# AdaLN block with attention: the scale product in column blocks, and the first projections accumulated by pairs of column tiles

## The reference

```python
mod = (_silu(L0_c) @ L0_wmod).reshape(4, 6, 1, -1)
sa, ca, ga, sb, cb, gb = (mod[:, i] for i in range(6))
ga = (2 * (ga >= 0) - 1) * jnp.maximum(jnp.abs(ga), 0.25)   # gb likewise
h = _layernorm(x, axis=-1) * (1 + ca) + sa
qkv = h @ Wqkv + bqkv                                       # 1024 -> 3 * 256
attn = softmax(q k^T / 16); out = (attn @ v) @ Wo + bo      # one head of 256
x = x + ga * out
h = _layernorm(x, axis=-1) * (1 + cb) + sb
x = x + gb * (h @ (weight + lora of this b).T + bias)       # 1024 -> 1024
```

## Time and profile before

| | us |
|---|---|
| median of 3 runs | 1041.43 (1040.65 to 1043.12) |
| the profiled execution | 1042.57 |
| its span in the profile | 1040.8 |
| TensorE busy | 1011.5 |
| VectorE busy | 663.6 |
| ScalarE busy | 309.2 |
| GpSimd busy | 231.2 |

### The profile page before, as it was taken

One profiled execution on the slowest core, in us unless ns is written; L12 is line 12 of the kernel. 1 busy time (PEld: TensorE's weight loads), 2 busy tenths in 40 slices (PEclk: granted clock), 3 DMA queues, 4 the chain that ended last, 5 costly groups with the idle time before them and its releaser, 6 DMA issues.

```text
span 1040.8 us, 12891 instructions
## 1 busy us (share of the span) xinstructions
PE 1011.5 (97%) x5158; PEld 831.6 (80%) x5158; DVE 663.6 (64%) x827; ACT 309.2 (30%) x460; POOL 231.2 (22%) x182
## 2 busy tenths in 40 slices
PE   4899999999999999999999999999999999999996
PEld 1677777888888889888898888888887888888885
DVE  4866756498744398532976548776688578566622
ACT  1422333123232132420234523322432333142300
POOL 0000000423201322004230034342223315042411
PEclk9899999999999999999999999999999999999999
DMA  9987574767102553024443146565553646463421
GB/s 348 409 317 244 211 295 140 252 227 265 70 1 77 207 197 127 1 94 157 155 162 117 41 142 225 203 220 184 200 202 126 216 145 202 140 225 122 142 76 66
DMA packets 54475, 180.74 MB, mean 174 GB/s; under 512 B 5784, under 2 KB 6352, under 8 KB 54416
## 3 DMA queue, kind: packets, MB, share of 16 engines
q1 hardware_dynamic: 45152, 146.35, 40.9%
q0 software_dynamic: 9104, 33.04, 8.4%
q10 hardware_dynamic: 160, 0.53, 0.1%
HBM read 146.25 MB, written 33.65 MB: 173 GB/s over the span
## 4 chain that ended last, share of the span: by engine, by line
PE 91%; DMA 4%; DVE 2%; SPq 1%; issue 1%; POOL 0%; ACT 0%; DVEq 0%; POOLq 0%; ACTq 0%
PE pairC L1370 8%; PE pairA L1370 8%; PE pairC L1371 8%; PE pairC L1372 7%; PE pairA L1371 7%; PE pairA L1372 7%; PE pairD L1370 7%; PE pairD L1371 7%; PE pairD L1372 7%; PE pairB L1370 5%; PE pairB L1371 5%; PE pairB L1372 5%; DMA z_cols<-in_x_cols 2%; PE pairB L1526 1%; PE pairD L1478 1%; PE pairA L1478 1%
## 5 line engine op out<-in xcount | busy, mean ns | idle before, releaser
L923 POOL TENSOR_TENSOR xr<-xr,row_bc 128x1024 f32<-128x1024 f32 x32 | 79.9, 2503 | 110.1 <-DMA xr<-in_x 90.3
L936 POOL TENSOR_TENSOR res<-res,row_bc 128x1024 f32<-128x1024 f32 x32 | 81.7, 2565 | 83.4 <-DMA res<-x_dram 76.9
L1370 PE MATMUL pairC<-w_hi,h_hi 128*128 128x512 f32 (+1 forms) x256 | 90.1, 352 | 0.0
L1371 PE MATMUL pairC<-w_lo,h_hi 128*128 128x512 f32 (+1 forms) x256 | 90.0, 351 | 0.0
L1372 PE MATMUL pairC<-w_hi,h_lo 128*128 128x512 f32 (+1 forms) x256 | 89.6, 350 | 0.0
L1370 PE MATMUL pairD<-w_hi,h_hi 128*128 128x512 f32 (+1 forms) x224 | 77.6, 346 | 0.0
L1371 PE MATMUL pairD<-w_lo,h_hi 128*128 128x512 f32 (+1 forms) x224 | 77.6, 346 | 0.0
L1372 PE MATMUL pairD<-w_hi,h_lo 128*128 128x512 f32 (+1 forms) x224 | 77.2, 345 | 0.0
L928 POOL DMA_DIRECT2D x_dram<-xr x32 | 18.0, 562 | 229.3 <-DVE xr L1276 229.3
L1079 ACT ACTIVATE w_hi<-w_sum 128x1024 fp32r<-128x1024 f32 x32 | 33.8, 1059 | 100.5 <-DVE w_sum L1320 100.2
L1370 PE MATMUL pairB<-w_hi,h_hi 128*128 128x512 f32 (+1 forms) x160 | 59.8, 374 | 0.0
(11 more groups left out here) (344 smaller groups left out, 2570.9 us busy)
## 6 DMA issues: line engine op xcount, KB each, us to landing
wm<-in_wmod SPq DMA_DIRECT2D x48, 512.0 KB, 6.4
xr<-in_x SPq DMA_DIRECT2D x34, 512.0 KB, 4.0
z_cols<-in_x_cols SPq DMA_DIRECT2D x32, 512.0 KB, 6.3
x_dram<-xr POOLq DMA_DIRECT2D x32, 512.0 KB, 3.8
xs<-x_dram SPq DMA_DIRECT2D x32, 512.0 KB, 4.7
w2t<-in_w2t SPq DMA_DIRECT2D x32, 512.0 KB, 4.3
res<-x_dram SPq DMA_DIRECT2D x32, 512.0 KB, 5.7
out_y<-res POOLq DMA_DIRECT2D x31, 512.0 KB, 3.5
```

The source lines that it names most:

```text
L923: nc.gpsimd.tensor_tensor(xt, xt, row_bc[:, :], ALU.add).then_inc(residual_made, 1)
L936: nc.gpsimd.tensor_tensor(rt, rt, row, ALU.add).then_inc(residual2_made, 1)
L1370: nc.tensor.matmul(out, left[0], right[0], start=first, stop=False)
L1371: nc.tensor.matmul(out, left[0], right[1], start=False, stop=False)
```

## The change

The part CA is taken in four blocks of 256 columns. `M0` c multiplies all eight row tiles by the columns of block c, in four groups of 32 partitions; `MC0` copies 256 columns; `MT0` turns them with two products; `MM0` adds 1 and writes the scale of one pair of column tiles. The transfers of CA change with it: transfer k brings 512 rows of wmod by 256 columns. For them the buffers wm lie by twos in one tensor. The counters mod_copied, mod_turned and mod_made count the other five parts only. `HH` of the first chunk waits for the scale of its own pair.

Keys, queries and values of the first chunk are all accumulated by pairs: `K0`, `Q0` and the new `V0`, with PSUM for all three open at once (keys in pair B, queries in D, values in A). The half weights come in the order keys, queries, values, keys, queries, values.

The spread is cut: `BCM` for the mean waits for the statistics alone, `BCP` for the reciprocal deviation, and ScalarE copies both to SBUF (`BMC`, `BPC`) before VectorE reads them. `SI` stands ahead of the first statistics in VectorE's list.

All five lists are new from one end to the other. Behind the first part the same steps stand in them, in another order.

```diff
-PARTS = ((1, 0), (1, 1), (0, 0), (0, 1), (2, 0), (2, 1))
+PARTS = ((1, 0), (0, 0), (2, 0), (1, 1), (0, 1), (2, 1))
 PE_ORDER = [
-    ("BCP", (), "A", None), ("M", (0, 0), "B", None), ("M", (0, 1), "B", None), ("M", (0, 2), "B", None),
-    ("M", (0, 3), "B", None), ("MT", (0,), "B", None), ("K0", (0,), "C", None), ("K0", (1,), "C", None),
-    ("K0", (2,), "C", None), ("K0", (3,), "C", None), ("V", (0, 0, 0), "D", None), ("M", (1, 0), "B", ("M", 0)),
...
+    ("BCM", (), "A", None), ("BCP", (), "A", None), ("M0", (0,), "B", None), ("MT0", (0,), "B", None),
+    ("M0", (1,), "C", None), ("MT0", (1,), "C", None), ("Q0", (0,), "D", None), ("M0", (2,), "A", ("BCM",)),
+    ("K0", (0,), "B", ("M0", 0)), ("MT0", (2,), "A", None), ("K0", (1,), "B", None), ("M0", (3,), "C", ("M0", 1)),
+    ("V0", (0,), "A", ("M0", 2)), ("V0", (1,), "A", None), ("MT0", (3,), "C", None), ("Q0", (1,), "D", None),
+    ("RT0", (0, 1), "C", ("M0", 3)), ("Q0", (2,), "D", None), ("M", (1, 0), "C", ("RT0", 0, 1)),
+    ("V0", (2,), "A", None), ("M", (1, 1), "C", None), ("V0", (3,), "A", None), ("Q0", (3,), "D", None),
+    ("M", (1, 2), "C", None), ("M", (1, 3), "C", None), ("K0", (2,), "B", None), ("K0", (3,), "B", None),
+    ("MT", (1,), "C", None), ("M", (2, 0), "A", ("V", 0, 0)), ("SAM", (), "C", ("M", 1)), ("M", (2, 1), "A", None),
+    ("SAT", (), "C", None), ("TWM", (), "C", ("SAM",)), ("M", (2, 2), "A", None), ("TWT", (), "C", None),
+    ("M", (2, 3), "A", None), ("K", (0, 1, 0), "B", ("K", 0, 0)), ("MT", (2,), "A", None),
...
 ACT_ORDER = [
+    ("WQH", (1, 0), None), ("BMC", (), "A"), ("BPC", (), "A"), ("WQH", (0, 0), None), ("MC0", (0,), "B"),
+    ("HH", (0, 0, 0), None), ("MC0", (1,), "C"), ("WQH", (2, 0), None), ("WQH", (1, 1), None),
+    ("HH", (0, 0, 1), None), ("MC0", (2,), "A"), ("WQH", (0, 1), None), ("WQH", (2, 1), None),
+    ("HH", (0, 0, 2), None), ("MC0", (3,), "C"), ("SC", (0, 1), "C"), ("SW", (0, 1), None), ("HH", (0, 0, 3), None),
+    ("LBC", (0, 1), None), ("VH", (0, 0, 0), "A"), ("VH", (0, 0, 1), "A"), ("MC", (1,), "C"),
+    ("HH", (0, 1, 0), None), ("HH", (0, 1, 1), None), ("HH", (0, 1, 2), None), ("HH", (0, 1, 3), None),
+    ("SAC", (), "C"), ("KH", (0, 0, 0), "B"), ("KH", (0, 0, 1), "B"), ("TWC", (), "C"), ("QH", (0, 0, 0), "D"),
...
 DVE_ORDER = [
+    ("SI", (), None), ("ST", (0, 0), None), ("ST", (0, 1), None), ("ST", (0, 2), None), ("ST", (0, 3), None),
+    ("WQL", (1, 0), None), ("Z", (0, 0, 0), None), ("WQL", (0, 0), None), ("MM0", (0,), "B"),
+    ("HL", (0, 0, 0), None), ("MM0", (1,), "C"), ("WQL", (2, 0), None), ("Z", (0, 0, 1), None),
+    ("WQL", (1, 1), None), ("HL", (0, 0, 1), None), ("Z", (0, 0, 2), None), ("MM0", (2,), "A"),
+    ("WQL", (0, 1), None), ("ST", (0, 4), None), ("ST", (0, 5), None), ("ST", (0, 6), None), ("ST", (0, 7), None),
+    ("MM0", (3,), "C"), ("HL", (0, 0, 2), None), ("Z", (0, 0, 3), None), ("WQL", (2, 1), None),
+    ("HL", (0, 0, 3), None), ("ST", (1, 0), None), ("VL", (0, 0, 0), "A"), ("VL", (0, 0, 1), "A"),
+    ("Z", (0, 1, 0), None), ("Z", (0, 1, 1), None), ("Z", (0, 1, 2), None), ("MM", (1,), "C"),
+    ("Z", (0, 1, 3), None), ("HL", (0, 1, 0), None), ("HL", (0, 1, 1), None), ("HL", (0, 1, 2), None),
+    ("BQ", (), "C"), ("ST", (1, 1), None), ("KL", (0, 0, 0), "B"), ("KL", (0, 0, 1), "B"), ("HL", (0, 1, 3), None),
...
 SP_ORDER = [
     ("LN", 0, 0), ("LN", 0, 1), ("Lsm",), ("LN", 0, 2), ("LN", 0, 3), ("Lid",), ("LWq", 1, 0), ("LT", 0, 0, 0),
+    ("Lwm", 0, 0), ("Lwm", 0, 1), ("LWq", 0, 0), ("LT", 0, 0, 1), ("Lwm", 0, 2), ("Lwm", 0, 3), ("LWq", 2, 0),
+    ("LT", 0, 0, 2), ("Lwm", 0, 4), ("Lwm", 0, 5), ("LWq", 1, 1), ("LWq", 0, 1), ("LT", 0, 0, 3), ("Lwm", 0, 6),
+    ("Lwm", 0, 7), ("LWq", 2, 1), ("LN", 0, 4), ("LN", 0, 5), ("LN", 0, 6), ("LN", 0, 7), ("LT", 0, 1, 0),
...
+                    if s == CA:
+                        half, at = k % 2, q * H + k // 2 * 2 * P
+                        src = wmod[half * BANK:(half + 1) * BANK, at:at + 2 * P].rearrange("(k p) n -> p k n", p=P)
+                        sp.dma_start(wm[k].rearrange("p (k n) -> p k n", k=4), src).then_inc(ld_wm[k], 16)
+                        return
...
+                elif what == "MC0":
+                    c = i[0]
+                    act.wait_ge(mod_used, 2 * c + 2)
+                    wait(act, ca_turned, c - 1)
+                    nc.scalar.activation(mod_rows[:, c % 2 * 2 * P:(c % 2 + 1) * 2 * P], ps[:, 0:2 * P], ACT.Copy).then_inc(ca_copied, 1)
+                elif what in ("BMC", "BPC"):
...
+                    cols = slice(0, CHUNK) if what == "BMC" else slice(CHUNK, 2 * CHUNK)
+                    nc.scalar.activation(bc[:, cols], ps[:, cols], ACT.Copy).then_inc(spread_copied, 1)
...
-                    act.wait_ge(mod_made, 1)
+                    act.wait_ge(ca_made, k + 1 if b + j == 0 else 4)
...
+                elif what == "M0":
+                    c = i[0]
+                    if c == 0:
+                        pe.wait_ge(c_ready, 1)
+                    for k in range(CT):
+                        if k % 4 == 0:
+                            pe.wait_ge(ld_wm[2 * c + k // 4], 16)
+                        q = 32 * (k % 4)
+                        last = nc.tensor.matmul(ps[q:q + 32, 0:2 * P], scT[:, k * B:k * B + 32],
+                                                wm[2 * c + k // 4][:, k % 4 * 2 * P:(k % 4 + 1) * 2 * P],
+                                                start=(k < 4), stop=(k >= 4))
...
+                elif what == "V0":
+                    c = i[0]
+                    pe.wait_ge(w_lo_made, PARTS.index((2, c // 2)) + 1)
+                    pe.wait_ge(h0_lo_made, 2 * c + 2)
+                    for ct in range(2 * c, 2 * c + 2):
+                        for t in range(4):
+                            last = product3(ps[:, t * D:(t + 1) * D], both(h_hi[0], h_lo[0], ct, slice(t * P, (t + 1) * P)),
+                                            both(w_hi, w_lo, ct, slice(2 * D, 3 * D)), ct == 0 and t % 2 == 0, ct == CT - 1)
```

More of the change, by code:

```diff
@@ L521, in build_block @@
             with ExitStack() as early:
-                wm = [sb(f"wm{i}", [P, H], at=early) for i in range(4)]
+                wm_pair = [sb(f"wm{i}", [P, 2, H], at=early) for i in range(2)]
             wo_hi = sb("wo_hi", [P, DT, H], F32R, at=first)
@@ L535, in build_block @@
             with ExitStack() as early:
-                wm += [sb(f"wm{i}", [P, H], at=early) for i in (4, 5, 6, 7)]
+                wm_pair += [sb(f"wm{i}", [P, 2, H], at=early) for i in (2, 3)]
             k_hi = sb("k_hi", [P, DT, S], F32R, at=first)
@@ L539, in build_block @@
             v_lo = sb("v_lo", [P, QT, D], F32R, at=first)
+        wm = [wm_pair[i // 2][:, i % 2, :] for i in range(8)]
         wo_raw = [xr, probs, probs, probs]
@@ L961, in step @@
                     act.wait_ge(mod_used, CT * (s + 1))
-                    wait(act, mod_turned, s)
+                    if s == SA:
+                        act.wait_ge(ca_turned, 4)
+                    else:
+                        act.wait_ge(mod_turned, s - 1)
                     if s == GA:
@@ L991, in step @@
                     act.wait_ge(st_stat, 16 * q)
+                    wait(act, z_made, 4 * q)
                     src = stats_dram[q].rearrange("k n -> (k n)").partition_broadcast(P)
@@ L1369, in product3 @@
             def product3(out, left, right, first, last):
-                nc.tensor.matmul(out, left[0], right[0], start=first, stop=False)
-                nc.tensor.matmul(out, left[0], right[1], start=False, stop=False)
-                return nc.tensor.matmul(out, left[1], right[0], start=False, stop=last)
+                nc.tensor.matmul(out, left[0], right[0], start=first, stop=False, skip_group_check=True)
+                nc.tensor.matmul(out, left[0], right[1], start=False, stop=False, skip_group_check=True)
+                return nc.tensor.matmul(out, left[1], right[0], start=False, stop=last, skip_group_check=True)
             def both(hi, lo, *where):
@@ L1383, in step @@
                         nc.tensor.matmul(ps[:, 0:BANK], w_hi[:, 0, D:D + P], w_hi[:, 0:2, D:2 * D], start=True, stop=True)
+                elif what == "M0":
+                    c = i[0]
[8 more added lines that the diff above has]
+                                                start=(k < 4), stop=(k >= 4))
+                        if k % 4 == 3:
+                            last.then_inc(mod_used, 1)
+                elif what == "MT0":
+                    c = i[0]
+                    pe.wait_ge(ld_const, 16)
+                    pe.wait_ge(ca_copied, c + 1)
+                    for cc in range(2):
+                        at, col = BANK + B * cc, c % 2 * 2 * P + cc * P
+                        last = nc.tensor.matmul(ps[:, at:at + B], mod_rows[:, col:col + P], sel, start=True, stop=True)
+                    last.then_inc(ca_turned, 1)
                 elif what == "M":
                     s, r = i
-                    if s + r == 0:
```

(20 more changed lines are left out.)

92 lines of the change are left out of this document (51 added, 41 removed), and 654 rows, old and new, of tables (ACT_ORDER, DVE_ORDER, PE_ORDER, POOL_ORDER).

## The result

| | before | after |
|---|---|---|
| median of 6 runs each on one chip, us | 1041.04 (1040.33 to 1043.12) | 1045.04 (1043.43 to 1045.78) |
| ratio | 1 | 1.0033 (95%: 1.0021 to 1.0044) |
| profiled execution, its span | 1042.57, 1040.8 | 1045.05, 1043.3 |

The ratio is estimated from all the runs and is not the quotient of the two medians, which lie 4.0 us apart (1.0038). On a second chip, 12 runs of the changed kernel gave 1.0026 (1.0013 to 1.0040). The change costs about 3 us (0.26 to 0.33%); 1044.7 was forecast.

A forecast was written before the change was run, and what follows sets the result against it. TensorE, busy 97%, was taken to bound the kernel. -4.7 + 2.7 + 1.0 + 1.35 = +0.35 us, with the clock +3.3: 1045.9 against the profiled execution, 1044.7 in runs; range 1037.5 to 1048.5.

The forecast's parts named there:

- The head: Up to the first query product: early sigmoid delays statistics to 14.9, yet the product starts at 25.9 us, 4.7 earlier.
- Moved and cut work: Behind the first product: scale blocks 2 and 3 cost 2.7 us, more cuts between products cost 1.0 us.
- The crowd's waits: Small steps gathered between the last keys and the next rows' keys: 1.55 us of waits against 0.2, +1.35.
- The fence's 0.3: At the end of the crowd: next keys wait 0.3 us for the last h_lo, behind one statistic and two k_lo.
- The clock: Half speed from about 80 to 89 us: 2.5 in the crowd, 2.1 in the keys, less 1.7 now, +2.9.
- Rival B: In the crowd of small steps: the clock is not let down; -1.35, 1040.1 us; chance 0.22.
- Total waits: TensorE over the whole span: waits some 3 us shorter than before, with the span not shorter.
- C: Rival at the start: the early start holds the clock as well, no half speed left; -3.9, 1037.5 us; chance 0.17.
- D: Rival in the scale's loads: 1 KB pieces cost twice the time; 4 us more, 1048.7 us; chance 0.07.
- The other end that I gave for a load: Scale's loads: 1 KB pieces cost 1.5 times, 1.92 us a load; effect on the time taken as 0.
- E: Rival behind 90 us: new order has waits, +2 to +4, clock holds in crowd; about 1043.5 us; chance 0.07.
- F: Rival at the first product: it waits as long as now for another operand; about 1041.5 us; chance 0.05.

The follow-up runs named there:

- e_si: Changed kernel with the sigmoid of c put back behind the four statistics; ratio 1.0015 to the kernel before.
- e_sp: Changed kernel with the last four loads of the gates' weights issued ahead of the next sequence's column loads; ratio 1.0006 to the kernel before.
- e_hot: Changed kernel with eleven overwritten products added in the waits of the crowd of small steps; ratio 1.0000 to the kernel before.
- e_dense: Changed kernel with the crowd opened by a pair of keys, bias steps behind quarters, gates' weights loaded first, last h_lo earlier; ratio 0.9992 to the kernel before.
- e_warm: Changed kernel with 15 overwritten products in TensorE's idle time ahead of the first query product; ratio 1.0020 to the kernel before.
- e_big: Changed kernel with the scale's eight loads in the old form, 4 KB pieces instead of 1 KB; 1044.76 us, ratio 1.0021 to the kernel before.
- a_same: The changed kernel itself, unchanged, run again on another chip; 1045.03 us, ratio 1.0026 to the kernel before.
- b_warm: Kernel before with ten overwritten products between the turn of the scale and the first keys; ratio 1.0007 to the kernel before.

## Why the prediction was right

**The head** held term by term: statistics 14.9 forecast and 14.8 measured, the spread's halves at 14.95 and 16.85 (14.83 and 17.09), first centring 19.45 (19.57), the scale 23.4 (23.27), first product 25.9 (25.87). `e_si` confirms that the early sigmoid delays the first product, but only by 1.1 of the 2.8 us named: the transfers of the second block would have been next. The prediction's point that near 23 would speak against late statistics was thus too coarse.

**Moved and cut work.** The view lists no wait between 25.9 and 75 us, and the shift was turned at 70.50 (70.6 forecast), so 2.7 + 1.0 us is right in sum.

**The crowd's waits.** 0.25 and 1.0 were forecast for the bias turn and the output bias product, 0.38 and 0.80 came. The fence's 0.3 did not. Missed was the 1.24 us for the weights of the gates' third quarter: the four column loads ahead of them in SP's list wait for the last products of the keys. I had followed TensorE, VectorE and ScalarE through the crowd and not SP's queue; `e_sp` shows the cause. The late weights cost more than that wait, as the quarter's two row tiles then ran one after the other: 3.21 instead of 1.94 us at 80.86.

**The clock.** Half speed was forecast from about 80 to 89 and came from 79.8 to 90.1. From the quarter's start to the next keys there are three steps of 1.0 us each at full clock; they took 6.8, so 3.8 more. The clock's part is 2.0 us by `e_hot` (6.8 against 4.8) or 2.5 if the 1.3 of the row tiles are taken off, where 2.5 was forecast; the rest, 1.3 to 1.8, is the late weights. Behind the next keys half speed cost 1.2 (2.4 us of products), where 2.1 was forecast. `e_hot` shows that this stretch is what makes the change slower: without it the change is level with the kernel before, with the waits for the weights still there. Rival B, no fall in the crowd at 1040.1, is that case, and the measured 1.0000 and 0.9992 (`e_dense`, where waits are gone too) put it at 1040.6 to 1041.4.

**The sum.** At the next keys the change stands 4.0 us later than before (87.67 against 83.67) with one turning of 0.9 owed; then 1.2 against 1.7 of half speed, and 0.4 against 1.2 us of waits behind 90 us, where I had taken them as equal: +3.6. The spans differ by 2.5. The remaining 1.1 us I could not place. That 1044.7 came so close to 1045.0 is in part luck: at the next keys the forecast was 1.9 us too early (87.67 against 83.3 and 2.5), since the late weights were missed, and behind them 0.9 too dear for the clock, 0.8 for the waits and 1.1 for what stays open.

**A sign that failed.** Total waits some 3 us shorter than before were forecast. The view lists 21.5 us against 19.7, so 1.8 longer. The 2.9 us ahead of the first product are gone, but TensorE's first step waits 1.1 longer for the statistics, the new head has waits of 2.7 and 1.0 for its copies, and the crowd has three. The prediction had most of these terms one by one and did not add them up to this total.

**The rivals.** C, full clock behind the start, did not happen by itself; where it was brought about, the ratio of `e_warm` fell by 1.3 us, within the noise, and not by 2.6. D, pieces twice as dear and 4 us, is refuted by `e_big` as to the time. The other end that I gave for a load, 1.5 times, was too high: by the 379 GB/s at 1.06 against 410 at 1.03 a byte of the mixed traffic costs 1.11 times. If wm is about half of it, its pieces cost about 1.2 times (an estimate). The Trainium skill ("DMA: Bandwidth & Descriptors", "Why small descriptors are slow (HBM only)") states a fixed overhead of about 3 cycles a packet beside its 32-byte beats. The 1.07 times estimated from it is below even the mixture's 1.11. E, waits of the new order behind 90 us, did not come (0.4 us against 1.2), and F falls with 25.87.

## What to carry to other kernels

An earlier start of the bottleneck engine is worth only what isn't moved behind it, and what the engines that feed it can follow: here 4.7 us became 1.0, and the waits ahead of the first product had not shrunk at all (18.7 us against 18.3). Small steps of TensorE, once spread between large products, should stay spread; gathered, they wait for one another's copies, and the clock falls on top (10.2 us at half speed, which cost 3.2 by the timeline of `e_hot`). Where steps are reordered, every queue must be walked through the new order, that of the transfers too, for an issue that stands behind one which waits.

## What was not expected of the hardware

- Eleven 512-column products into a bank that is overwritten later made a kernel faster, not slower, where the clock would have fallen (`e_hot`: 2.7 to 3.4 us). Fifteen in the head gave no gain clear of the noise (`e_warm`).
- Where stretches of half speed begin and end differs between executions of one program: after the start it lasted 6.8 us in the changed kernel, and 3.4 in `e_sp`, `e_hot` and `e_big`, which are the same there but for the form of the transfers in the last. In the crowd it was 10.2 us in the changed kernel and 13.7 in `e_big`. Every stretch seen was 3.4, 6.8, 10.2 or 13.7 us long. Runs of one kernel spread over 2 to 8 us, so that 12 runs of each leave about 0.1%. In `a_same` the spread goes with the clock: the fastest run, 1040.83 us, has the highest mean, 0.994, and the slowest, 1048.88, one of 0.988.
- Half speed in the head seems to cost less than half its length: taking it away gave 1.3 us of 3.1 (`e_warm`, within the noise), and `b_warm`, which had full speed up to the thirteenth product and half speed for 3.4 us behind it, gained 0.4 us up to that product and nothing in the time.
